# Node stage of a graph kernel: the addition of the attention rows moves from GpSimd to VectorE

## What is computed

```python
xn = _layernorm(x)
out1 = segment_sum(edge_attr, col)        # per node: sum of its edges
out2 = segment_max(edge_attr, col)        # maximum, 0 for a node without edges
out3 = out1 / max(cnt, 1)                 # mean
h = concatenate([xn, out1, out2, out3, u[batch]])
gnn = relu(h @ W1 + b1) @ W2 + b2 + xn
x = x + gnn + mix(xn)                     # mix: an attention-like layer, linear in n
x = x + ffn(_layernorm(x))                # ffn only for the 3124 rows of the highest score
```

## Time and profile before

| | us |
|---|---|
| runs | 1412.85 median of 3 (1408.34 to 1413.47) |
| the profiled execution | 1419.74 |
| its span, first to last instruction | 1418.0 |
| TensorE / VectorE / ScalarE / GpSimd busy | 1090.3 / 1003.8 / 466.5 / 492.5 |
| GpSimd additions (L1279), 13 | 41.1 |
| mean granted clock of TensorE | 0.864 of full speed |

### The profile page before, as it was taken

The page is one execution under the profiler, slowest core; times in us unless marked ns, Lnnn a source line. Parts: engine busy times, 40 slices in busy tenths (PEclk is TensorE's granted clock), DMA queues, the critical chain, the costliest instruction groups (busy, mean ns, idle before and its releaser), DMA issues. The chain is left out here.

```text
span 1418.0 us, 17209 instructions
## 1 busy us (share of the span) xinstructions
PE 1090.3 (77%) x5137; PEld 825.1 (58%) x5137; DVE 1003.8 (71%) x2336; ACT 466.5 (33%) x1392; POOL 492.5 (35%) x389
## 2 busy tenths in 40 slices
PE   2287998989953751389988898889889941599998
PEld 1144454545532530277877687778778840488887
DVE  5999969979999984567756775577558447545452
ACT  4256665757521322113212321232123221122231
POOL 0078818800000005766434643464343002222221
PEclk9598999999966975599998998899989975599997
DMA  9699988979978965524344524352442120211110
GB/s 327 241 333 320 333 324 298 334 303 326 332 279 300 413 235 151 173 67 142 90 126 114 153 75 125 111 155 76 124 117 98 55 101 13 61 40 52 57 52 17
DMA packets 97828, 249.79 MB, mean 176 GB/s; under 512 B 13241, under 2 KB 62789, under 8 KB 91492
## 3 DMA queue, kind: packets, MB, share of 16 engines
q1 hardware_dynamic: 50946, 165.89, 32.0%
q0 software_dynamic: 17968, 41.34, 12.1%
q10 hardware_dynamic: 28850, 41.83, 8.3%
HBM read 162.15 MB, written 86.85 MB: 176 GB/s over the span
## 5 line engine op out<-in xcount | busy, mean ns | idle before, releaser
L1504 ACT ACTIVATE hT_hi<-psH 128x512 fp32r<-128x512 f32 (+1 forms) x104 | 59.7, 574 | 285.6 <-PE psH L1573 264.6
L49 PE MATMUL psO<-W2s_hi,hT_hi 128*128 128x256 f32 (+1 forms) x392 | 124.4, 317 | 16.7 <-issue 16.3
L51 PE MATMUL psO<-W2s_hi,hT_lo 128*128 128x256 f32 (+1 forms) x392 | 120.2, 307 | 21.1 <-issue 20.9
L50 PE MATMUL psO<-W2s_lo,hT_hi 128*128 128x256 f32 (+1 forms) x392 | 119.6, 305 | 19.6 <-issue 19.5
L941 POOL DMA_INDIRECT graw<-in_edge_attr,ic x98 | 115.7, 1180 | 42.4 <-issue 26.9
L460 DVE SCALAR_TENSOR_TENSOR ob<-ob,mQ,mx 128x96 f32<-128x96 f32 x392 | 122.2, 312 | 7.1 <-DVE xb L451 3.7
L463 DVE SCALAR_TENSOR_TENSOR ob<-ob,kQ,xb 128x96 f32<-128x96 f32 x392 | 122.1, 311 | 0.7 <-issue 0.7
L299 POOL DMA_INDIRECT near<-ends_d,blki x49 | 87.7, 1790 | 88.6 <-DVEq L417 74.0
L1378 DVE TENSOR_TENSOR x<-bg,psO 128x256 f32<-128x256 f32 (+1 forms) x49 | 20.7, 422 | 136.4 <-remote 69.8
L1279 POOL TENSOR_TENSOR bg<-bg,tg 128x1024 f32<-128x1024 f32 (+1 forms) x13 | 41.1, 3166 | 213.5 <-DMA tg<-att_d 213.4
L803 PE MATMUL psQ<-Wqk,xT 128*128 128x512 f32 (+1 forms) x196 | 100.6, 637 | 0.0
(11 more groups left out here) (401 smaller groups left out, 2993.7 us busy)
## 6 DMA issues: line engine op xcount, KB each, us to landing
xb<-in_edge_attr SPq DMA_DIRECT2D x49, 1536.0 KB
scan_d<-ob SPq DMA_DIRECT2D x49, 768.0 KB
yrow_d<-yr SPq DMA_DIRECT2D x12, 1040.0 KB
xg<-in_x ACTq DMA_DIRECT2D x12, 512.0 KB
xT_d<-xT ACTq DMA_DIRECT2D x12, 512.0 KB
base_d<-dcur ACTq DMA_DIRECT2D x12, 512.0 KB
qT_d<-qT ACTq DMA_DIRECT2D x12, 512.0 KB
xTr<-xT_d SPq DMA_DIRECT2D x12, 512.0 KB, 3.5
```

Of the source, the lines that this page charges most:

```text
L49: nc.tensor.matmul(out, lh, rh, start=start, stop=False)
L50: nc.tensor.matmul(out, lh, rl, start=False, stop=False)
L51: return nc.tensor.matmul(out, ll, rh, start=False, stop=stop)
L1504: nc.scalar.activation(hT[0][:, m, 0:n], psH[m % 4][:, 0:n], ACT.Relu).then_inc(s_rh, 1)
```

## The change

GpSimd no longer adds: it copies indices and issues gathers only, each of which waits for nothing but the aggregates of the group two before. VectorE does the same addition, once per group, in the turn of that group, behind relu_low(5) and ahead of part 1 of `finish` for the group before. It waits for the same loads and raises the same semaphore s_bsum.

```diff
@@ gpsimd @@
-                def add_attention(g, e, n):
-                    nt, rows = shape(g)
-                    pool.wait_ge(s_lb[e], n)
-                    nc.gpsimd.tensor_tensor(bg[e][0:rows, 0:nt, :], bg[e][0:rows, 0:nt, :], tg[e][0:rows, 0:nt, :], ALU.add).then_inc(s_bsum, 1)
-
                 gather(1, 1)
-                add_attention(0, 0, 32)
-                add_attention(1, 1, 32)
-
-                gather(2, 0)
-                add_attention(2, 0, 64)
-                gather(3, 1)
-                add_attention(3, 1, 64)
+                for g in range(2, 4):
+                    gather(g, g % 2)
                 with pool.Fori(2, 6) as h:
                     for e in range(2):
                         gather(h * 2 + e, e)
-                        add_attention(h * 2 + e, e, h * 32 + 32)
                 gather(GROUPS, 0)
-                add_attention(GROUPS, 0, 7 * 32)
@@ vector @@
+                def add_attention(g, e, h):
+                    nt, rows = shape(g)
+                    dve.wait_ge(s_lb[e], h * 32 + 32)
+                    nc.vector.tensor_tensor(bg[e][0:rows, 0:nt, :], bg[e][0:rows, 0:nt, :], tg[e][0:rows, 0:nt, :], ALU.add).then_inc(s_bsum, 1)
...
                         relu_low(g, m)
                         if m < 5 and nxt:
                             aggregate(g + 1, 1 - e, h + e, m)
+                        if m == 5:
+                            add_attention(g, e, h)
                         if m == GT - 2 and (not isinstance(g, int) or g >= 1):
                             deviation(g - 1)
                         if m >= GT and (not isinstance(g, int) or g >= 1):
```

## The result

| | before | after |
|---|---|---|
| median of 4 runs each, us | 1411.72 (1408.34 to 1413.47) | 1426.25 (1421.12 to 1432.14) |
| the profiled execution | 1419.74 | 1423.50 |
| GpSimd busy, us | 492.5 | 435.7 |

The account below looks back on a forecast made before the run. The prediction took slow stretches of TensorE's output phase, 7.9 to 8.4 us a turn plus recovery, to bound the node stage. Turns 1 to 8, 0 and 9 summed to 41+17-9 = +49: 1412.85+49 = 1462 us, range 1385 to 1495.

Parts of the forecast that it names:

- The stretch: In output matmuls of turns 1 to 9, TensorE slows to a trickle while gathers run, losing 7.9 to 8.4 us.
- the two stores: SP's two stores per turn, at the same place as now, share DMA engines with the moved gathers; 8 us allowed for sharing.
- Turn 9: Only group 12's four gathers remain, over by +33.6, so hardly a stretch: 9 us less.
- the stretch begins at +31.9: In turns 1 to 8 the slow stretch starts 31.9 us into the turn, 7.6 into output; 5.1 us more per turn.
- The last term, 6.2 us: After the slow stretch, each turn's other 31 output instructions run at the low clock, 0.2 us each: 6.2 us.
- an onset at +34: Alternative start of the slow stretch, 34 us into the turn: 2.3 us more per turn, total 1439.
- turn 0: First turn's output meets early gathers, is slow from about 621.6 and ends at about 656, not 639: 17 us more.
- rival A: Stretch begins a fixed time after the first gather, at +38, after output ends; turns 1 to 9 shorten: 1349; chance 0.18.
- Rival B: Stretch keeps its length and only moves, into hidden matmuls if need be: no change, 1413, within 7; chance 0.18.
- the store at 804.89: SP's DMA instruction in turn 4 takes 0.70 us, longer than most; taken as a sign that more than TensorE is slowed.
- Rival C: Gathers don't matter; VectorE is the hidden limit and 1.9 us per turn come back: 21 us, 1392; chance 0.04.
- Rival D: VectorE's addition makes the last relu_low late by 1.2 us in 12 turns: 15 us, 1428; chance 0.04.

Follow-up runs that it names:

- a1: Kernel after, addition still on VectorE, but gathers held near their old place by a wait for the previous group's loads; 1325.39 us, 1.0000 to the kernel before.
- c1: The same kernel as a1, sent again in another set: addition on VectorE, gathers near their old place; 0.9983 to the kernel before.
- d1: The kernel after, unedited, run again in a set without stretches; 1.0005 to the kernel before.
- b1: The kernel after, unedited, run again in another set, with stretches; 1433.32 us, 1.0149 to the kernel before.
- b2: The kernel before, unedited, a single run for its trace in a set with stretches; 1412.36 us.

## Why the prediction was wrong

**Right:** the direction, and the way to it. The stretch bounds the turn, it moves with the gathers, and it ends with them: 2.4 us behind the last issue against some 2. The first gather was placed at +23.4 and came at +22.4 (850.63 less 828.20). The row took 22.2 us and the stretch ended at +47.0, where +46 was taken. The addition was priced at 1.2 us and took 1.21, without a wait; it costs nothing on the path (a1, c1, d1, all without stretches, and the 0.51 us that the last relu_low waits for ScalarE). No run prices the two stores or the sharing of DMA engines by themselves. Turn 9 was to give back 9 us and gave 9.7.

**The step that failed first: "the stretch begins at +31.9".** It was drawn from two turns, as a time in the output phase that shrinks by 0.3 us per us. In turns 3 to 8 the count fits instead, and it gives more: with some 78 to 90 matmuls to run, mostly at 0.12 us, turn 5's stretch began at +34.7, 9.7 us into output. It held 79 matmuls before, not 62; 22 trickled, not 15; and 12 were left at the end, not 31. The last term, 6.2 us, measured 2.3. So turn 5 ended at +49.3, not +52.2, and turns 1 to 8 cost 2.6 us each on average, not 5.1: 20.9 us in place of 41. That average owes much to turn 3, whose extra stretch in the hidden matmuls no term foresaw. The bound with an onset at +34 had priced a turn at 2.3 us more, and two turns' onsets were enough to see that a count fits them as well as a slope does (both rows of before say 86).

**The step that failed second: turn 0,** 17 us more by the forecast, and 7.3 less in fact. "By the same rule is slow from about 621.6" is what it rested on. In fact had a gather at 607.24 and no stretch until 626.1, which was held against rival A and should have been held against the forecast's rule too. Its start for gather(3) was wrong too: that came at 627.84, not 622, as gather(2) took 26.2 us to issue, and its stretch began at 643.3, when turn 0 had been over for 11 us. Why gather(2), from 600.66, brings no stretch is not known. Turn 0 is 24 us of the 45 by which the sum missed this execution, and turns 1 to 8 are 20.

The measured terms are 20.9 - 7.3 - 9.7 = +3.9 for this execution. This pair understates the change: the execution of before took 8.0 us more than its kernel's median, that of after 2.8 less, and 3.76 + 8.02 + 2.75 is the 14.5 between the medians. b1 against b2 gives 16.7, and turn 1 of b1, with 53.3 us, is alone 5.7 longer than that of after.

**Rival A** fell: output phases of turns 4 to 8 were not over when the stretch came, 10.5 to 12.3 us after the first gather and not 15. **Rival B** was half right: stretches do reach hidden matmuls (721.7 to 731.2, 15 matmuls in 9.5 us), so "it slowed nothing while TensorE ran hidden matmuls" held for the row that it was read from, not for all; but their length doesn't stay, 12 us where before had 8. That more than TensorE is slowed was right, but the store at 804.89 is thin evidence. It begins 1.3 us ahead of TensorE's stretch, and that of turn 5 took 0.40 us; in a1 all twelve take 0.37 to 0.41. **Rival C** fell: the stalls of 1.9 us are gone (VectorE is 7 us less busy with 13 additions more) and in d1 the whole is worth 1.0005. The Trainium skill's rule for the shared port ("SBUF — State Buffer", section "Who interferes with whom") is borne out by the durations and decides nothing, as VectorE is not the bound. The same page's statement that DMAs and engines cannot conflict agrees with d1, where TensorE ran at full pace beside a DMA share of 0.83; in after TensorE stalls while a row of gathers is issued, by a way that the statement doesn't cover and no row names. **Rival D** fell with the 0.51 us.

## The version that beats both

The changed kernel with its gathers split into tiles (a3, c3, d2, e1) takes 1324 to 1326 us in every set. Against the kernel before that is 0.9408 (0.9385 to 0.9431) where the stretches show, and 0.9995, 0.9987 and 0.9997 where none do, with intervals that all hold 1. The kernel after, compared in its own sets, is at 1.0094 and 1.0149 with stretches. So the version is better than both where there are stretches (one set of four runs) and equal where there are none. What makes it better is not known.

## What to carry to other kernels

When work moves off an engine, ask first what was queued behind it: here the addition showed in no time, and what the change did was to let 16 gathers go 10 us later in the turn, into other company. Long rows of indirect DMAs issued without a step between are worth a trial cut into fours with a wait in each. Here it cost nothing (waits for TensorE's progress) or 0.2% (waits for landed gathers) where it wasn't needed, and gave 6% where it was. And an idle time put down to "issue" deserves a count (how many instructions since the suspect began) beside a clock: two turns fitted a wrong slope in time, and the count was in the same rows. Look at the other engines in the same microseconds too, before calling them followers.

## What was not expected of the hardware

- The same program takes 1326 or 1412 us depending on the set it runs in, always alike within one: 86 us of stretches, in which TensorE issues single matmuls or short bursts with gaps of up to 2.6 us (before) and no semaphore to wait for the earlier trace rows.
- The other engines are held too: ScalarE and VectorE took up finished tiles some 9 us after their matmuls in turn 4 of before (0.5 and 1.6 us in a1), and in turn 1 of after ScalarE was late while TensorE still ran at full pace.
- The stretch outlasts the trickle in price. The granted clock is 0.68 in the stretch and 0.51 in the 2.3 us behind it in turn 5 of after, the lower of the two levels (1.2 GHz). Where the stretch ended earlier, as in turn 4 of before, 69 matmuls paid for it, at 0.72.
- No rule in the rows covers every case. One kernel's row of 16 gathers beside 138 matmuls passed without a gap (e1), others' brought one after 86, or after 110 and more in early turns. In turn 0 of after 212 matmuls ran without a gap beside gathers in one row.
